# An expert-routed four-layer chain on one core: PE's preparation reordered, routing products among the warm-up products, and one group of linear products moved ahead of layer 1's last down product, with one DVE instruction of layer 4 moved up

## The reference, cut to what matters

```python
x = x + L0(x, cond_8)   # expert = argmax of the 8 values; silu(x Wu + bu) * (x Wg + bg), then Wd + bd
x = x + L1(x, cond_8)   # x W_base + b + 2 * sum over the 8 experts of w[b,e] * (x As[e]) Bs[e], rank 16
x = x + L2(x, cond_8)   # weights = sum over 8 groups of y[b,g] * weight[g] * mask; plus bias
x = x + L3(x, cond_8)   # top-2 experts of softmax: gated gelu MLP with 512 hidden, plus one shared MLP
```

## Time and profile before

| | us |
|---|---|
| median of 3 runs | 155.03 |
| profiled execution, its own time | 154.85 |
| its span, from the first to the last instruction | 152.8 |
| PE busy | 148.2 |
| DVE busy | 110.3 |
| POOL busy | 91.5 |
| ACT busy | 72.1 |

### The profile page before, as it was taken

One profiled execution on the slowest core, in us unless ns is written; L12 is line 12 of the kernel. 1 busy time (PEld: TensorE's weight loads), 2 busy tenths in 40 slices (PEclk: granted clock), 3 DMA queues, 4 the chain that ended last, 5 costly groups with the idle time before them and its releaser, 6 DMA issues.

```text
span 152.8 us, 3109 instructions
## 1 busy us (share of the span) xinstructions
PE 148.2 (97%) x1075; PEld 134.5 (88%) x1075; DVE 110.3 (72%) x229; ACT 72.1 (47%) x138; POOL 91.5 (60%) x93
## 2 busy tenths in 40 slices
PE   7999999999999999999999999999999999999992
PEld 2269999999986999999989999999999999999881
DVE  2886676666896686768876868785587886968772
ACT  2866444452374554544463454545435334346540
POOL 1002999999700005939994949996785999880000
PEclk9999999999999999999999999999999999999999
DMA  3989999994363667294296567086538048000052
GB/s 78 399 264 355 405 410 402 409 416 158 142 231 89 179 163 257 33 311 144 54 324 209 177 236 230 14 263 239 188 101 309 6 116 296 6 0 0 0 207 71
DMA packets 13911, 30.15 MB, mean 197 GB/s; under 512 B 1336, under 2 KB 8008, under 8 KB 13768
## 3 DMA queue, kind: packets, MB, share of 16 engines
q1 hardware_dynamic: 13472, 28.76, 54.5%
q10 hardware_dynamic: 424, 1.20, 2.1%
HBM read 24.71 MB, written 1.05 MB: 169 GB/s over the span
## 4 chain that ended last, share of the span: by engine, by line
PE 86%; DVE 4%; POOL 3%; DMA 2%; ACT 2%; issue 1%; SPq 0%; ACTq 0%; DVEq 0%; POOLq 0%
PE pair L543 22%; PE pair L533 12%; PE acc L592 10%; PE pair L480 9%; PE pair L550 8%; PE acc L577 6%; PE acc L488 5%; PE acc L601 5%; PE pair L447 3%; PE pair L469 2%; PE pair L519 2%; PE pair L512 2%; POOL duo_lo L371 2%; DVE hid L765 2%; DMA lora_sb<-lora 2%; ACT hid_hi L430 2%
## 5 line engine op out<-in xcount | busy, mean ns | idle before, releaser
L371 POOL TENSOR_TENSOR duo_lo<-raw_duo,duo_hi 128x512 fp32r<-128x512 f32 x36 | 48.7, 1352 | 2.9
L756 DVE TENSOR_TENSOR hid_lo<-hid,hid_hi 128x512 fp32r<-128x512 f32 (+1 forms) x41 | 36.5, 892 | 18.0 <-ACT hid_hi L430 17.2
L430 ACT ACTIVATE hid_hi<-hid 128x512 fp32r<-128x512 f32 (+1 forms) x41 | 25.4, 622 | 44.2 <-DVE hid L765 41.2
L368 POOL CAST duo_hi<-raw_duo 128x512 fp32r<-128x512 f32 x36 | 28.4, 788 | 29.1 <-PE acc L592 29.1
L765 DVE TENSOR_TENSOR hid<-pair,act 128x512 f32<-128x512 f32 (+1 forms) x49 | 32.9, 674 | 5.7 <-PE pair L543 4.1
L543 PE MATMUL pair<-x_duo,duo_hi 128*128 128x256 f32 x192 | 35.3, 282 | 0.4 <-issue 0.3
L411 ACT ACTIVATE act<-pair 128x512 f32<-128x512 f32 x48 | 28.4, 591 | 10.1 <-PE pair L543 8.1
L543 PEld LDWEIGHTS pair<-x_duo,duo_hi 128*128 128x128 f32 x192 | 29.6, 188 | 1.4 <-DVE hid L765 0.7
L543 PE MATMUL pair<-x_duo,duo_lo 128*128 128x256 f32 x96 | 26.9, 280 | 0.0
L533 PE MATMUL pair<-x_hl,shared_hi 128*128 128x512 f32 x64 | 20.5, 402 | 0.0
L543 PEld LDWEIGHTS pair<-x_duo,duo_lo 128*128 128x128 f32 x96 | 18.0, 188 | 0.0
(11 more groups left out here) (95 smaller groups left out, 198.1 us busy)
## 6 DMA issues: line engine op xcount, KB each, us to landing
raw_duo<-experts SPq DMA_DIRECT2D x12, 768.0 KB, 5.0
ring<-experts SPq DMA_DIRECT2D x16, 386.5 KB, 6.9
raw_solo<-experts SPq DMA_DIRECT2D x8, 768.0 KB, 5.1
x_duo<-x_hl SPq DMA_DIRECT2D x24, 128.0 KB, 3.5
x<-xT ACTq DMA_DIRECT2D x1, 1024.0 KB, 6.4
lora_raw<-x SPq DMA_DIRECT2D x4, 256.0 KB, 2.4
raw_solo<-shared SPq DMA_DIRECT2D x1, 768.0 KB, 8.9
out<-lora_raw SPq DMA_DIRECT2D x3, 256.0 KB, 2.8
```

The costliest lines, as they stand in the source:

```text
L368: pool.tensor_copy(duo_hi[:, j % HALVES, piece(n)], raw_duo[:, j % RAWS, piece(n)])\
L371: pool.tensor_tensor(duo_lo[:, j % HALVES, piece(n)], raw_duo[:, j % RAWS, piece(n)], duo_hi[:, j % HALVES, piece(n)].bitcast(F32), ALU.su ...
L430: act.activation(hid_hi[:, k % SPLITS, at], hid3[:, u % PAIRS, at], ACT.Copy)\
L756: dve.tensor_tensor(hid_lo[:, k % SPLITS, at], hid3[:, u % PAIRS, at], hid_hi[:, k % SPLITS, at].bitcast(F32), ALU.subtract).then_inc(hid_ ...
```

## The change

1. The warm-up products are split: five, then the `at_diag` product, one, then the two rank products, two, and only then the four `prepare1` (the first of which stood ahead of the `at_diag` product before).
2. DVE copies `at_row` ahead of its first `bs_w` instruction, no longer between the second and the third.
3. The preparation rotates through three banks, `pair[1][0]`, `pair[1][1]`, `acc[0]`, where it had two; each step now waits for the copy of three steps back. The rank products go to `pair[2][0]`, and layer 1 alternates between `pair[0]` and `pair[2]` in place of `pair[0]` and `pair[1]`.
4. Layer 2's first group of four products (`linear1(0)`, into `pair[1][0]`) stands between upgate0(15) with down0(14) and down0(15); the other three groups follow down0(15) as before.
5. At the start of layer 4 DVE does low_part(3) ahead of hidden_low(0), no longer behind it.

```diff
--- before.py
+++ after.py
@@ -197,7 +197,8 @@
                 for p in range(PAIRS)]
         acc = [ctx.enter_context(nc.psum_tensor(f"acc{n}", [P, N], F32)) for n in range(2)]
         lin = pair[1] + pair[2]
-        prep = pair[2]
+        prep = pair[1] + acc[:1]
+        layer1 = [pair[0], pair[2]]
 
         cond_in, rep_in, lora_in = sem("cond_in"), sem("rep_in"), sem("lora_in")
         small_in, w2_in = sem("small_in"), sem("w2_in")
@@ -392,12 +393,12 @@
                 else:
                     k = 2 * (n - G)
                     dst = mix_raw[:, k:k + 2, :, :].rearrange("p k b j -> p (k b j)")
-                act.activation(dst, prep[n % 2][:, :], ACT.Copy).then_inc(prep_copied, 1)
+                act.activation(dst, prep[n % 3][:, :], ACT.Copy).then_inc(prep_copied, 1)
 
             for b in range(B):
                 act.wait_ge(up0_done, b + 1)
                 for c in range(C0):
-                    act.activation(act0[:, b % FREE, c, :], pair[b % FREE][0][:, c * P:(c + 1) * P], ACT.Silu,
+                    act.activation(act0[:, b % FREE, c, :], layer1[b % FREE][0][:, c * P:(c + 1) * P], ACT.Silu,
                                    bias=ring0[:, b % SLOTS0, BUP0 + c:BUP0 + c + 1]).then_inc(act0_done, 1)
             act.preload_act_table(ACT.Gelu_apprx_tanh)
 
@@ -437,27 +438,28 @@
                     pe.matmul(acc[0][:, :].rearrange("p (b n) -> p b n", n=P), zeros[:, :],
                               zeros[:, :].unsqueeze(1).to_broadcast([P, GB, P]), start=True, stop=True)
 
-            pe.wait_ge(zeros_set, 1)
-            warm(8)
-
             def prepare1(q):
                 pe.wait_ge(bsw_done, q + 1)
-                if q >= 2:
-                    pe.wait_ge(prep_copied, q - 1)
-                pe.matmul(prep[q % 2][:, :], lora_sb[:, AS1:AS1 + P],
+                if q >= len(prep):
+                    pe.wait_ge(prep_copied, q - len(prep) + 1)
+                pe.matmul(prep[q % 3][:, :], lora_sb[:, AS1:AS1 + P],
                           bs_w[:, q * GB:(q + 1) * GB, :].rearrange("p b o -> p (b o)"),
                           start=True, stop=True).then_inc(prep_mm, 1)
 
-            prepare1(0)
+
+            pe.wait_ge(zeros_set, 1)
+            warm(5)
             pe.wait_ge(ones_set, 3)
             pe.wait_ge(at_diag_done, 1)
             pe.matmul(acc[1][:, 0:B], ones_b[:, :], at_diag[:, :], start=True, stop=True).then_inc(at_mm, 1)
+            warm(1)
 
             pe.wait_ge(chosen_done, 1)
-            pe.matmul(pair[1][0][0:B, 0:E], earlier_b[:, :], chosen_b[:, :], start=True, stop=True)
-            pe.matmul(pair[1][0][0:B, E:2 * E], ones_b[:, 0:B], chosen_b[:, :], start=True, stop=True)\
+            pe.matmul(pair[2][0][0:B, 0:E], earlier_b[:, :], chosen_b[:, :], start=True, stop=True)
+            pe.matmul(pair[2][0][0:B, E:2 * E], ones_b[:, 0:B], chosen_b[:, :], start=True, stop=True)\
               .then_inc(rank_mm, 1)
-            for q in range(1, G):
+            warm(2)
+            for q in range(G):
                 prepare1(q)
 
             pe.wait_ge(ydelta_done, 1)
@@ -465,8 +467,8 @@
             for k in range(E):
                 n = G + k // 2
                 if k % 2 == 0:
-                    pe.wait_ge(prep_copied, n - 1)
-                ins = pe.matmul(prep[n % 2][:, (k % 2) * B * R:(k % 2 + 1) * B * R], w2_sb[:, k, :],
+                    pe.wait_ge(prep_copied, n - len(prep) + 1)
+                ins = pe.matmul(prep[n % 3][:, (k % 2) * B * R:(k % 2 + 1) * B * R], w2_sb[:, k, :],
                                 y_delta[:, :, :].rearrange("p b j -> p (b j)"), start=True, stop=True)
                 if k % 2 == 1:
                     ins.then_inc(prep_mm, 1)
@@ -477,7 +479,7 @@
                     pe.wait_ge(hid0_done, (b - FREE + 1) * C0)
                 for half, (base, done) in enumerate(((UP0, up0_done), (GATE0, gate0_done))):
                     for c in range(C0):
-                        ins = pe.matmul(pair[b % FREE][half][:, c * P:(c + 1) * P],
+                        ins = pe.matmul(layer1[b % FREE][half][:, c * P:(c + 1) * P],
                                         ring0[:, b % SLOTS0, base + c * P:base + (c + 1) * P],
                                         x[:, cols(b)], start=True, stop=True)
                     ins.then_inc(done, 1)
@@ -488,6 +490,13 @@
                     ins = pe.matmul(acc[b % 2][:, 0:P], ring0[:, b % SLOTS0, DOWN0 + c * P:DOWN0 + (c + 1) * P],
                                     hid0[:, b % FREE, c, :], start=(c == 0), stop=(c == C0 - 1))
                 ins.then_inc(down0_done, 1)
+
+            def linear1(g):
+                pe.wait_ge(x1_done, GB * g + GB)
+                for j in range(GB):
+                    ins = pe.matmul(lin[g][:, j * P:(j + 1) * P], lin1[:, g * GB + j, :],
+                                    x[:, cols(g * GB + j)], start=True, stop=True)
+                ins.then_inc(lin_mm, 1)
 
             pe.wait_ge(x_in, 16)
             upgate0(0)
@@ -500,18 +509,16 @@
             for b in range(B):
                 if b + 1 < B:
                     upgate0(b + 1)
+                else:
+                    pe.wait_ge(lin1_done, G)
+                    linear1(0)
                 if b == FREE:
                     pe.wait_ge(slots_done, 2)
                     solo_batch = values(mybir.EngineType.PE, slot_row[0:1, 2 * DUOS:SLOTS])
                 down0(b)
 
-            pe.wait_ge(lin1_done, G)
-            for g in range(G):
-                pe.wait_ge(x1_done, GB * g + GB)
-                for j in range(GB):
-                    ins = pe.matmul(lin[g][:, j * P:(j + 1) * P], lin1[:, g * GB + j, :],
-                                    x[:, cols(g * GB + j)], start=True, stop=True)
-                ins.then_inc(lin_mm, 1)
+            for g in range(1, G):
+                linear1(g)
             pe.wait_ge(lin2_done, E)
             for g in range(G):
                 pe.wait_ge(lin_read, g + 1)
@@ -637,11 +644,10 @@
                                       cond_sb[:, IOTA:IOTA + E].unsqueeze(1).to_broadcast([B, K, E]), ALU.is_equal))
             dve.tensor_tensor(chosen_b[:, :], onehot[:, 0, :], onehot[:, 1, :], ALU.add).then_inc(chosen_done, 1)
             dve.wait_ge(rep_in, 16)
+            dve.wait_ge(at_mm, 1)
+            dve.tensor_copy(at_row[:, :], acc[1][0:1, 0:B]).then_inc(at_done, 1)
             dve.wait_ge(lora_in, 16)
             for q in range(G):
-                if q == 2:
-                    dve.wait_ge(at_mm, 1)
-                    dve.tensor_copy(at_row[:, :], acc[1][0:1, 0:B]).then_inc(at_done, 1)
                 at = slice(q * GB, (q + 1) * GB)
                 dve.scalar_tensor_tensor(
                     bs_w[:, at, :], lora_sb[:, BS1:BS1 + P].unsqueeze(1).to_broadcast([P, GB, P]), LORA_SCALE,
@@ -664,7 +670,7 @@
 
 
             dve.wait_ge(rank_mm, 1)
-            chained(dve.tensor_copy(rank_n[:, :], pair[1][0][0:B, 0:2 * E]))
+            chained(dve.tensor_copy(rank_n[:, :], pair[2][0][0:B, 0:2 * E]))
             rank = rank_n[:, 0:E]
             chained(dve.tensor_tensor(reached[:, :, :], rank_n[:, E:2 * E].unsqueeze(2).to_broadcast([B, E, B]),
                                       cond_sb[:, EVENS:EVENS + B].unsqueeze(1).to_broadcast([B, E, B]), ALU.is_ge))
@@ -701,7 +707,7 @@
                 for c in range(C0):
                     dve.wait_ge(act0_done, b * C0 + c + 1)
                     dve.scalar_tensor_tensor(
-                        hid0[:, b % FREE, c, :], pair[b % FREE][1][:, c * P:(c + 1) * P],
+                        hid0[:, b % FREE, c, :], layer1[b % FREE][1][:, c * P:(c + 1) * P],
                         ring0[:, b % SLOTS0, BGATE0 + c:BGATE0 + c + 1], act0[:, b % FREE, c, :], ALU.add, ALU.mult)\
                        .then_inc(hid0_done, 1)
 
@@ -792,8 +798,8 @@
 
             product(0)
             low_part(2)
+            low_part(3)
             hidden_low(0)
-            low_part(3)
             product(1)
             hidden_low(1)
             for u in range(2, UNITS + 2):
```

## The result

| | before | after |
|---|---|---|
| median, us | 155.28 (4 runs, 154.92 to 155.67) | 153.69 (4 runs, 153.31 to 154.58) |
| ratio after / before, 95% interval | | 0.9914 (0.9886 to 0.9942) |
| profiled execution, its own time | 154.85 | 153.69 |
| its span | 152.8 | 151.7 |

By the ratio the change is 0.86% faster, 1.33 us of 155.28 (the two medians differ by 1.59), beyond the 0.5% that a measurement can tell. Forecast were 153.65 us and -1.38.

A forecast was written before the change was run, and what follows sets the result against it. PE, busy 148.2 of 152.8 us, was taken to bound the kernel, so only its idle or held-up places count. Terms -0.57 - 0.30 - 0.51 = -1.38 take 155.03 to 153.65 us; range 153.2 to 154.8.

The forecast's parts named there:

- Term A: Before layer 1: PE's preparation 0.78 us faster, but a new 0.21 wait for payload leaves -0.57 us.
- x and the loads: Before layer 1: earlier ring loads may delay x to 11.2, still ahead of PE's need at 11.5; cost taken as 0.
- Term B: End of layer 1: linear products fill PE's wait for hidden values; last down product 0.75 to 0.45, -0.30 us.
- Term C: Start of layer 4: earlier gathers remove idle and slow duo start, one down product gains, another loses; -0.51 us.
- Rival 1: Before layer 1 payload is not late, -0.78, and layer 4 gains its bound -0.71: 153.2 us; chance 0.10.
- Rival 2: Gain shrinks downstream in layer 4, or late small_sb swallows the gain before layer 1: 154.1 to 154.7 us; chance 0.22.
- Rival 3: Before layer 1: PE's clock still at 1.2 GHz, up to 160.4 us; chance 0.08 together with x or first expert late.
- Rivals 4 and 5: Layer 1: x or first expert late (0.08 with Rival 3); whole kernel: no tellable effect (inside Rival 2's 0.22).

The follow-up runs named there:

- e2_linear: The kernel before with the banks swapped (preparation still on two) and linear group 0 ahead of the last down product; 155.18 us, ratio 0.9992.
- e3_low: The kernel before with only low_part(3) moved ahead of hidden_low(0) at the start of layer 4; 154.20 us, ratio 0.9942.
- e8: The changed kernel with two banks in the preparation in place of three; 154.31 us, ratio 0.9951.
- e9: The changed kernel with DVE's copy of at_row back between the second and third bs_w; 153.98 us, ratio 0.9914.
- e7: The changed kernel with six warm-up products, the last two gone; median 155.14 us in 12 runs that fall into two groups.

## Why the prediction was right

The time (153.69 for 153.65) and the direction are right, and the 1.33 us of the ratio lie within 0.1 of the 1.38 forecast. The steps:

- **Term A, before layer 1: -0.57 forecast, -0.51 found between the two profiles and about -0.63 over all executions (the estimate above), by another way than I said.** I named a new wait of 0.21 for `payload`. There is none: payload is done at 12.02, PE comes to the slot products at 12.76. The step that failed is that `small_sb` lands at 6.62 and `y_delta` can start only at 6.72; it started at 6.09. That landing was an accident of the one trace: in the twelve profiles taken since, it came 3.7 to 4.1 after its issue, also with the old code (3.9 in e2_linear, 3.8 in e3_low). The second error went the other way: "three small products cost about 0.2 in all". Eight warm-ups from 1.01 on end at 4.43, and the first `prepare1` starts at 4.88, so they cost 0.45. The gaps that I had put below 0.1 each are 0.17 before the `at_diag` product (3.15 to 3.32) and 0.11 before the rank products. The two errors cancel but for 0.06. The rest held: the pace of 6.91 us for eight steps (6.89 from 5.05 to 11.94 in the chain), no stop for copies (e8 shows what it was worth), `at_row` early and worth nothing by itself (e9).
- **x and the loads**: x landed 6.2 us after its issue in the changed kernel, 6.4 before, although the loads came 2.2 us earlier. In the other profiles with early loads it was 6.2 to 7.6, at most 10.0 on the time line, and layer 1 started at 11.63 or later. So the turn-taking of the queues that the Trainium skill describes (DMA: Bandwidth & Descriptors, Queues, rings and completion order) is compatible with the upper values, and no start of layer 1 was set by it.
- **Term B, edit 4: -0.30 forecast, -0.33 found in U to L, and +0.30 given back in L to S.** The failed step is the sentence "DVE's reads of the groups start 0.3 earlier likewise", together with "POOL starts behind the slot products, so 0.57 earlier too": I moved both and did not ask how they then stand to each other. DVE was clear of POOL's last instruction by nothing before (POOL until 41.20, low_part(0) from 41.08 and still at 0.68), so any shift of DVE forward against POOL had to meet it. The lower bound of zero that I gave for B is what happened, by a mechanism that I had not named.
- **Term C, edit 5: -0.51 forecast, -0.56 found.** The idle 0.28, the slow start (1.64 to 1.41) and the second down product's 0.20 went as written, the first down product pays 0.13 and not 0.20. The gathers start at 45.15; I had said 44.8.
- **The sum**: without the loss that I missed it would have been -1.40 on the spans, with it -1.10; with the 0.63 for term A it would be about -1.2. The ratio says -1.33, but no two executions have the same start of the clock, and that moves each by up to 1.3 us; so I don't read the difference between -1.10 and -1.33. The agreement with -1.38 to 0.05 is luck of the same kind.
- **Rival 1** (payload in time) was the true picture of the wait, and gave not its -0.78, for the start at 4.88. **Rival 2** (the gain shrinks downstream) is true of term B, with POOL for its cause. **Rival 3** (the clock) was not decisive for this change, but its mechanism is real and its price is about right: in e7's profile four `prepare1` instructions cost 1.90 us more (3.78 for 1.88), where I had said 1.7, and in e7 eight of twelve executions end at 154.97 or later, where the changed kernel's latest of ten is 154.58. It was at work in the kernel before already, which one trace could not show. **Rivals 4 and 5** did not occur.

## What to carry to other kernels

When an edit moves one engine forward, list what the other engines do at the new moment, and not only who waits for it: here the first instruction that DVE did earlier met POOL's last, and the whole gain of a well-found hole was gone. A term that looks lost is best looked for by cutting the span at marks: the stretches between the marks behind layer 1's start repeat to 0.01 to 0.04 us where the code is the same, while the times scatter by 1.3, so an effect of 0.3 us is plain in one profile and hard to see in twelve runs. And a landing time or a clock that one trace shows is one draw; a rival that rests on it deserves its chance.

## What the runs showed of the hardware

- A DVE TENSOR_TENSOR of 128x512 f32 with both operands in SBUF took 0.95 to 0.99 us (seven profiles) when it started 0.39 to 0.45 us before the recorded end of a POOL TENSOR_TENSOR, and 0.68 when it started 0.08 to 0.12 before it or later (six profiles). In after, POOL ends at 40.69 and DVE's instruction at 41.23, 0.54 later; in all seven it is 0.54 to 0.56. Before, it was 0.56 as well (41.20 and 41.76): there was no room. The Trainium skill (SBUF — State Buffer, Who interferes with whom) says that DVE and GpSimd share a pair of ports, which only one of them holds at a time, and that a DVE instruction with two SBUF inputs contends with a GpSimd instruction that reads SBUF. These rows agree: the loss was 0.27 to 0.31 us, and at this place it fell on that instruction alone; its neighbours on DVE, which read one operand from PSUM (L730, 0.75 apart), ran at their usual time beside POOL. In layer 4 it happens too, before as after: the changed kernel's `hidden_low` at 60.84, also with both operands in SBUF, took 1.28 instead of 0.69 beside POOL. I could have looked for it with that page.
- The clock of PE rises from 1.2 to 2.4 GHz at a moment that differs from one execution to the next: the first four `prepare1` instructions took 1.88 or 2.69 us in two executions of the same kernel, and 1.88 to 2.92 in the seven profiles with this order on PE and eight warm-ups. With two warm-up products fewer they took 3.78 in the one profile. The PEclk column stood at 1.00 there all the same.
- Small interruptions of PE cost more than the idle time that the rows show: three small products between warm-ups cost 0.45 us, the wait for `at_diag` among it, and a duo group behind an idle 0.28 took 1.64 instead of 1.41. What the 0.23 is made of is not shown.
